# A graph attention layer on one core: edge blocks gathered once into a ring, sums scaled once a group, one-hots shared by two engines, own rows added later

## The chip, the cores and the metric

The kernel runs on one core of one Trainium2 chip. The metric is the device time of one execution in microseconds. The engines are PE (TensorE; PEld is its weight load), DVE (VectorE), ACT (ScalarE), POOL (GpSimd) and SP (SyncE, which here only starts transfers); each has an instruction queue of its own, and they meet at semaphores. A queue is named with a q behind the engine (DVEq: the register instructions of DVE's queue).

## The reference

```python
xn = layer_norm(x, ln1_g, ln1_b)                     # 6250 nodes, 256 columns
h = (xn @ W).reshape(N, 8, 32)
a_src, a_dst = einsum(h, att_src), einsum(h, att_dst)
src, dst = edges + (i, i) for every node i           # 100000 sorted by dst, and the node's own row
e = leaky_relu(a_src[src] + a_dst[dst], 0.2)
ee = exp(e - segment_max(e, dst)[dst])
agg = segment_sum(h[src] * ee / segment_sum(ee, dst)[dst], dst)
out = layer_norm(agg + xn @ W_res + bias, ln2_g, ln2_b)
x = x + out + gelu(out @ ffn_w1 + ffn_b1) @ ffn_w2 + ffn_b2
x = x + top-2-of-8 experts(layernorm(x))             # weights from softmax(x @ Wr + br)
```

The destinations are drawn as 6250 u^2 with u uniform, so the low-numbered nodes have most of the edges.

## The kernel before, in words

There are four stages, one behind the other: the node stage (norm, `h`, the table `node_table` of 272 columns per node: eight heads of 32 values and a one, and eight `a_src`), the edge stage, the layer (merge, second norm, the two products of the small network, routing, the rows sent to the experts' buffers) and the experts. Only the first three are touched.

The edge stage works on the 391 blocks of 256 sorted edges (NEB). A block's destinations lie in windows of 128 nodes (49 of them, NT); a block that reaches into a further window is handled again for that one. One block with one window is a step; there are 440 steps in 55 groups of eight (GS, NG), and the steps come in order. For each step POOL gathers the block's 256 source rows as two indirect transfers of 128 rows (L768) into one of four group buffers `gath`. The other engines turn in a round, one group each time. The iteration of `edges_dve` with number g does on DVE: the node chain of g (new maxima of the eight windows, the split of the values into `parts`), woven with the eight sums of group g-1: the sum in `win_mem` is scaled (L1044), then PE's product of one-hot and message is added (L1048). Then a piece of the expert weights is split (L1140), the scan over group g+1's scores (L1059, L1061) is made, the scores of g (L1066 to L1070), and the messages of g: gathered rows times weights (L1023), in pieces of four tiles; the last four tiles follow one by one among the sums. ACT copies `a_src` out of the gathered rows (L855), makes the one-hots (sixteen L862, L865), turns the places into the other one-hot (L868, L872), takes the exponentials (L889) and widens the one-hot (L897). PE does the sums (L957), a residual product (L834, L835), the spread of node values to edges (L926) and the maxima (L944).

A sum starts from the node's own row of the table, which lies in `win_mem` from the node stage.

In the layer, a batch is four windows of 128 nodes (two smaller ones at the end, 13 batches). POOL's queue holds for each batch b the root of the merged rows two batches on (L418), the eight row transfers of batch b-2 (L1346), and the root of the new rows (L1335). DVE turns that root into factors (L1508), ACT applies them (L1270) and then goes on with the gelus of the next batch (L1260, L1261), for which PE has three banks.

A value load reads a number out of the memory into a register of an engine's queue; it is a TENSOR_LOAD followed by FUSED_REGOPS and SEQ_ASSERT. `edges_dve` has one in each round (L966), whose number holds the eight windows of the group.

## Time and profile before

| | |
|---|---|
| time, median of 3 runs | 2292.91 us (2291.22 to 2293.44) |
| the profiled execution's own time | 2291.67 us |
| its span, first to last instruction | 2290.4 us |
| mean granted TensorE clock | 0.856 |
| node stage, edge stage, layer, experts (by the trace) | 0 to 96, 96 to 1252, 1252 to about 1620, to 2290 us |

The difference between the span and the profiled execution's time is 1.3 us and stays. Busy shares are a mean over stages with different limits, so the stages are read one at a time. A shift of a few us in 2292.91 is about what a measurement tells from nothing.

### The profile page before, as it was taken

What the parts mean: (1) busy time and instruction counts of PE and PEld (TensorE: products, weight loads), DVE (VectorE), ACT (ScalarE), POOL (GpSimd) and SP (SyncE); (2) the same over time, 40 slices, a digit from 0 to 9 for tenths busy, and PEclk for the clock granted to TensorE, in tenths of its full rate; (3) what the DMA queues carried; (4) which work ended last, traced back from release to release, by engine and by line L of the source; (5) the groups of instructions that cost most, each with busy time, mean ns of one, the idle gap of its engine ahead of it and who ended that gap; (6) DMA issues with size and microseconds to landing.
All of it is one profiled execution on the core that took longest, in us unless ns stands there. A gap on an engine that the chain in (4) does not pass through costs nothing.

```text
span 2290.4 us, 43652 instructions
## 1 busy us (share of the span) xinstructions
PE 1796.5 (78%) x12962; PEld 1538.9 (67%) x12962; DVE 1745.3 (76%) x5414; ACT 1556.3 (68%) x3225; POOL 1184.8 (52%) x1168
## 2 busy tenths in 40 slices
PE   6537666676666677766666899999399999999998
PEld 4425545555545455555544788889399999999997
DVE  7349999899899899989998788887455555555554
ACT  3366777777677777676772787887377766666675
POOL 3377777777777777777770134445222222222223
PEclk9857777777777777777777999999699999999999
DMA  7867666767666667766664223322835356436432
GB/s 228 209 184 215 215 210 197 207 216 215 214 205 203 208 214 215 225 200 200 204 207 136 74 91 98 101 78 75 253 48 122 48 118 159 87 48 158 85 48 38
DMA packets 283231, 358.12 MB, mean 156 GB/s; under 512 B 118629, under 2 KB 227006, under 8 KB 280562
## 3 DMA queue, kind: packets, MB, share of 16 engines
q1 hardware_dynamic: 218578, 202.63, 28.7%
q0 software_dynamic: 63840, 151.61, 26.0%
q8 instruction: 104, 1.70, 0.3%
q10 hardware_dynamic: 576, 1.09, 0.2%
q14 instruction: 133, 1.09, 0.1%
HBM read 464.93 MB, written 95.79 MB: 245 GB/s over the span
## 4 chain that ended last, share of the span: by engine, by line
PE 46%; POOL 21%; issue 11%; DVE 11%; ACT 6%; DMA 4%; DVEq 0%; SPq 0%; POOLq 0%; ACTq 0%
POOL edge_mem L768 21%; PE bank L1156 8%; PE bank L1144 7%; PE bank L1145 7%; PE bank L1146 7%; PE bank L957 6%; PE bank L1155 4%; DMA edge_mem<-node_table,src_col 3%; ACT edge_mem L862 3%; DVE layer_rounded L1140 1%; PE bank L1153 1%; ACT edge_mem L868 1%; DVE edge_mem L1023 1%; PE bank L523 1%; PE bank L834 1%
## 5 line engine op out<-in xcount | busy, mean ns | idle before, releaser
L768 POOL DMA_INDIRECT edge_mem<-node_table,src_col x880 | 840.5, 955 | 277.2 <-issue 261.7
L957 PE MATMUL bank<-edge_mem 128*128 128x264 f32 x1760 | 524.1, 459 | 6.3 <-ACT edge_mem L897 3.3
L957 PEld LDWEIGHTS bank<-edge_mem 128*128 128x128 f32 x1760 | 382.9, 226 | 110.1 <-issue 26.3
L1886 POOL DMA_INDIRECT out<-expert_mem,slot_tok x112 | 174.4, 1557 | 488.4 <-DVE expert_mem L1823 468.5
L1873 ACT ACTIVATE expert_mem<-bank,par 128x256 f32<-128x256 f32 x448 | 221.8, 495 | 187.6 <-PE bank L1146 187.5
L1140 DVE TENSOR_TENSOR expert_rounded<-expert_mem,expert_rounded 128x512 fp32r<-128x512 f32 x280 | 193.6, 691 | 194.6 <-ACT expert_rounded L1873 121.9
L1023 DVE TENSOR_TENSOR edge_mem<-edge_mem,bank 128x1056 f32<-128x1056 f32 x385 | 293.9, 776 | 7.5 <-ACT bank L889 1.7
L1156 PE MATMUL bank<-expert_rounded 128*128 128x512 f32 x784 | 278.8, 395 | 0.0
L1144 PE MATMUL bank<-expert_rounded 128*128 128x256 f32 x896 | 254.6, 284 | 27.1 <-DVE expert_rounded L1140 27.1
L862 ACT ACTIVATE edge_mem<-iota,dst_col 128x128 bf16<-128x128 bf16 x880 | 262.8, 386 | 0.0
L1145 PE MATMUL bank<-expert_rounded 128*128 128x256 f32 x896 | 254.4, 284 | 0.0
L1146 PE MATMUL bank<-expert_rounded 128*128 128x256 f32 x896 | 254.3, 284 | 0.0
L855 ACT COPY asrc<-edge_mem 128x128 f32<-128x128 f32 x55 | 16.4, 298 | 308.8 <-DMA edge_mem<-node_table,src_col 308.8
L1873 ACT ACTIVATE expert_rounded<-bank,par 128x256 fp32r<-128x256 f32 x448 | 222.2, 496 | 0.0
L1155 PE MATMUL bank<-expert_rounded 128*128 128x256 f32 x784 | 218.5, 279 | 0.0
L926 PE MATMUL bank<-parts,edge_mem 128*128 128x16 bf16 x2640 | 77.8, 172 | 155.2 <-DVE parts L1015 155.2
L1048 DVE TENSOR_TENSOR win_mem<-win_mem,bank 128x264 f32 x440 | 187.2, 426 | 13.1 <-PE bank L957 12.5
L1144 PEld LDWEIGHTS bank<-expert_rounded 128*128 128x128 f32 x896 | 172.5, 193 | 27.4 <-issue 25.0
L1044 DVE TENSOR_TENSOR win_mem<-win_mem,bank 128x264 f32 x440 | 186.6, 424 | 4.5 <-issue 1.7
L926 PEld LDWEIGHTS bank<-parts,edge_mem 128*128 128x128 bf16 x2640 | 72.8, 101 | 170.1 <-DVE parts L1015 170.1
L1145 PEld LDWEIGHTS bank<-expert_rounded 128*128 128x128 f32 x896 | 172.6, 193 | 2.4
L1146 PEld LDWEIGHTS bank<-expert_rounded 128*128 128x128 f32 x896 | 172.6, 193 | 0.0
(245 smaller groups left out, 4240.6 us busy)
## 6 DMA issues: line engine op xcount, KB each, us to landing
expert_rounded<-split_w SPq DMA_DIRECT2D x114, 2048.0 KB
edge_mem<-step_place SPq DMA_DIRECT2D x55, 512.0 KB, 5.4
split_w<-piece_hi SPq DMA_DIRECT2D x72, 256.0 KB, 4.8
split_w<-piece_lo SPq DMA_DIRECT2D x72, 256.0 KB, 6.0
piece_full<-in_L_ffn_W SPq DMA_DIRECT2D x64, 256.0 KB
expert_mem<-expert_rows SPq DMA_DIRECT2D x224, 64.0 KB, 2.8
edge_mem<-node_table,src_col POOLq DMA_INDIRECT x880
node_table<-win_mem SPq DMA_DIRECT2D x12, 544.0 KB, 4.4
```

The source lines that it names most:

```text
L768: pool.indirect_dma_start(gath[g % NGB][:, t, :], None, node_table, bass.IndirectOffsetOnAxis(ap=src_col[:, k, t % 2:t % 2 + 1], axis=0)). ...
L862: ins = act.activation(o16[:, t, :], iota16[:, :], ACT.Abs, scale=-1.0, bias=dst_col[:, k, t % 2:t % 2 + 1])
L957: ins = pe.matmul(bank[4 + at % 3][:, 0:AGG], onehot[g % 2][:, 2 * k + j, :], gath[g % NGB][:, 2 * k + j, 0:AGG], start=(j == 0), stop=(j ...
L1023: dve.tensor_tensor(rows_, rows_, wgt[:, r, :].unsqueeze(3).to_broadcast([P, end - first_, HEADS, HC]), ALU.mult).then_inc(weighted, 1)
L1048: dve.tensor_tensor(acc, acc, bank[4 + at % 3][:, 0:AGG], ALU.add).then_inc(added, 1)
L1140: return eng.tensor_tensor(lo, full, hi.bitcast(F32), ALU.subtract)
L1144: pe.matmul(out_ap, s_hi, m_lo, start=start, stop=False)
L1145: pe.matmul(out_ap, s_lo, m_hi, start=False, stop=False)
L1146: return pe.matmul(out_ap, s_hi, m_hi, start=False, stop=stop)
L1155: pe.matmul(out_ap[:, 0:n], s_lo, high, start=False, stop=False)
L1156: return pe.matmul(out_ap, s_hi, both_, start=False, stop=stop)
L1873: ins = act.activation(d, bank[1 + m % 4][:, 0:SLOT], ACT.Gelu, bias=par[jf % 3][:, 2 * KC + m:2 * KC + m + 1])
```

## The change

- `gath` becomes a ring of 28 blocks (RB), found by tables that DVE makes in the node stage. A block is gathered once: 782 transfers in 98 quads of four blocks (QUAD), where there were 880. POOL reads from a table, before each quad from the eighth on, how many steps must have been weighted, and waits for that count.
- Messages go to a buffer of their own, `message`, step by step, since a block may be needed twice. DVE and ACT find a step's block by two words loaded for each group.
- A window's weights in a group are all made with the maxima after that group, so only the first window's sum is scaled, once a group. `win_mem` is set to zero at the start.
- DVE makes half of the one-hots (one comparison over eight tiles), ACT the other half.
- The own rows are read again from the table in the layer, weighted and added by `add_self`: batch 0 on DVE, the others on POOL.
- The source rows of the tables are loaded by plain transfers, not by four indirect ones; the first product's weights of the layer (`layer_w1`) are loaded after the last messages.

```diff
+    RB = 28
+    QUAD = 4
+    NQUAD = -(-NEB // QUAD)
...
-        gath = [part(i * GT * ROW, GT, ROW) for i in range(NGB)]
+        ring = part(0, 2 * RB, ROW)
+        message = part(2 * RB * ROW, GT, AGG)
...
+                dve.memset(rows_s[:, :, :], 0.0).then_inc(tables_made, 1)
...
-                    pool.indirect_dma_start(rows_s[:, c, :].bitcast(I32), None, src_rows, at).then_inc(rows_gathered, 16)
...
+                dve.wait_ge(pool_const, 13)
+                t = step(dve.tensor_tensor(block_of, block_of, win_row[:, :], ALU.subtract))
+                dve.wait_ge(dve_step, t)
+                t = step(dve.tensor_scalar(lap_of, block_of, float(-(-65536 // RB)), None, ALU.mult))
...
-            for g in range(NG):
-                if g == 2:
+            pool.wait_ge(tables_made, 5)
+            for q in range(NQUAD):
+                if q == 2 * GS // QUAD:
                     turned_all(pool)
-                for t in range(GT):
-                    if g >= 2 and t % QUART == 0:
-                        if t == QUART:
-                            pool.wait_ge(asrc_turned, g - 1)
-                        if t == 2 * QUART:
-                            pool.wait_ge(cand_turned, g - 1)
-                        if t == 3 * QUART:
-                            pool.wait_ge(maxima_made, g - 1)
-                    if g >= NGB and t % QUART == 0:
-                        pool.wait_ge(summed, GS * (g - NGB) + (GS // 2 if t < 2 * QUART else GS))
-                    k = g * GS + t // 2
-                    pool.indirect_dma_start(
-                        gath[g % NGB][:, t, :], None, node_table,
-                        bass.IndirectOffsetOnAxis(ap=src_col[:, k, t % 2:t % 2 + 1], axis=0)).then_inc(gathered[g % NGB], 16)
+                if q >= RB // QUAD:
+                    done = pool.value_load(reuse_at[0:1, q - RB // QUAD + 1:q - RB // QUAD + 2], min_val=1, max_val=NSTEP)
+                    pool.wait_ge(weighted, done)
+                    pool.sem_inc(pool_step, 1)
+                    pool.wait_ge(pool_step, q - RB // QUAD + 1)
+                if q >= 2:
+                    pool.wait_ge(gathered[q % 2], 32 * QUAD * (q // 2))
+                for j in range(q * QUAD, min((q + 1) * QUAD, NEB)):
+                    for i in range(2):
+                        pool.indirect_dma_start(
+                            ring[:, 2 * (j % RB) + i, :], None, node_table,
+                            bass.IndirectOffsetOnAxis(ap=src_col[:, j, i:i + 1], axis=0)).then_inc(gathered[q % 2], 16)
...
-                    if n >= 1:
-                        act.wait_ge(asrc_turned, n)
-                    act.copy(asrc[:, :, :, :], gb[:, :, :, AGG:ROW].rearrange("p k j h -> p j k h")).then_inc(asrc_ready, 1)
+                    slots = slot_words(act, n)
+                    if n < 2:
+                        for i in range(2):
+                            act.wait_ge(gathered[i], 32 * QUAD * (n + 1))
+                    else:
+                        landed = [act.value_load(landed_at[0:1, n, i:i + 1], min_val=1, max_val=32 * QUAD * NQUAD) for i in range(2)]
+                        for i in range(2):
+                            act.wait_ge(gathered[i], landed[i])
+                    if n >= 2:
+                        act.wait_ge(asrc_turned, n - 1)
+                        act.wait_ge(scored, n - 1)
+                    for k in range(GS):
+                        t = step_tile(slots, k)
+                        ins = act.copy(asrc[n % 2][:, :, k, :], ring[:, bass.ds(t, 2), AGG:ROW])
+                    ins.then_inc(asrc_ready, 1)
                     o16 = onehot16[n % 2]
                     if n >= 2:
                         act.wait_ge(maxima_made, n - 1)
                         act.wait_ge(oh_wide, n - 1)
-                    for t in range(GT):
+                    for t in range(GT // 2, GT):
                         k = n * GS + t // 2
                         ins = act.activation(o16[:, t, :], iota16[:, :], ACT.Abs, scale=-1.0, bias=dst_col[:, k, t % 2:t % 2 + 1])
                     ins.then_inc(act_step, 1)
                     act.wait_ge(act_step, n + 1)
-                    act.activation(o16, o16, ACT.Relu, scale=-1.0, bias=ones[:, 0:1]).then_inc(oh_ready, 1)
+                    act.activation(o16[:, GT // 2:GT, :], o16[:, GT // 2:GT, :], ACT.Relu, scale=-1.0, bias=ones[:, 0:1]).then_inc(oh_ready, 1)
...
-            if k == 0 or piece_of(2 * k + 1) != piece_of(2 * k - 1):
-                pe.wait_ge(weighted, NM * g + piece_of(2 * k + 1) + 1)
+            if k % 2 == 0 and k < EARLY:
+                pe.wait_ge(weighted, GS * g + k + 2)
+            if k >= EARLY:
+                pe.wait_ge(weighted, GS * g + k + 1)
             if at >= 3:
                 pe.wait_ge(added, at - 2)
             for j in range(2):
-                ins = pe.matmul(bank[4 + at % 3][:, 0:AGG], onehot[g % 2][:, 2 * k + j, :], gath[g % NGB][:, 2 * k + j, 0:AGG],
+                ins = pe.matmul(bank[4 + at % 3][:, 0:AGG], onehot[g % 2][:, 2 * k + j, :], message[:, 2 * k + j, :],
...
+            def weigh(g, k, first_, end):
+                if k == 0 and first_ == 0:
                     dve.wait_ge(weights_ready, g + 1)
-                dve.tensor_tensor(rows_, rows_, wgt[:, r, :].unsqueeze(3).to_broadcast([P, end - first_, HEADS, HC]), ALU.mult).then_inc(weighted, 1)
+                if (g, 0) not in words:
+                    words[g, 0] = slot_words(dve, g)
+                t = step_tile(words[g, 0], k)
+                return dve.tensor_tensor(message[:, 2 * k + first_:2 * k + end, :].rearrange("p t (h c) -> p t h c", c=HC),
+                                         ring[:, bass.ds(t + first_, end - first_), 0:AGG].rearrange("p t (h c) -> p t h c", c=HC),
+                                         wgt[:, 2 * k + first_:2 * k + end, :].unsqueeze(3).to_broadcast([P, end - first_, HEADS, HC]), ALU.mult)
+
+            def early_messages(g, m):
+                for k in (2 * m, 2 * m + 1):
+                    weigh(g, k, 0, 2).then_inc(weighted, 1)
+
+            def late_message(g, i):
+                ins = weigh(g, EARLY + i // 2, i % 2, i % 2 + 1)
+                if i % 2 == 1:
+                    ins.then_inc(weighted, 1)
...
-                            messages(p, 3 + k)
+                            late_message(p, k)
                             next(small, None)
                         w = window(p, k)
                         acc = win[:, w, 0:AGG]
                         acc_h = acc.rearrange("p (h c) -> p h c", c=HC)
                         if at:
                             dve.wait_ge(added, at)
-                        t_scaled = step(dve.tensor_tensor(acc_h, acc_h, scale[:, k, :].unsqueeze(2).to_broadcast([P, HEADS, HC]), ALU.mult))
+                        if k == 0:
+                            t_scaled = step(dve.tensor_tensor(acc_h, acc_h, scale.unsqueeze(2).to_broadcast([P, HEADS, HC]), ALU.mult))
                         next(small, None)
-                        dve.wait_ge(dve_step, t_scaled)
+                        if k == 0:
+                            dve.wait_ge(dve_step, t_scaled)
                         dve.wait_ge(summed, at + 1)
...
+                    if n >= 2:
+                        dve.wait_ge(maxima_made, n - 1)
+                        dve.wait_ge(oh_wide, n - 1)
+                    targets = dst_col[:, n * GS:n * GS + GS // 2, :].rearrange("p k j -> p (k j)")
+                    dve.tensor_tensor(onehot16[n % 2][:, 0:GT // 2, :], iota16[:, :].unsqueeze(1).to_broadcast([P, GT // 2, P]),
+                                      targets.unsqueeze(2).to_broadcast([P, GT // 2, P]), ALU.is_equal).then_inc(oh_half, 1)
...
-                    dve.wait_ge(gathered[g % NGB], 16 * GT * (g // NGB + 1))
-                    t = step(dve.tensor_tensor(score[:, :, :], gb[:, :, AGG:ROW], b_edge[:, :, 0:HEADS], ALU.add))
+                    dve.wait_ge(asrc_ready, g + 1)
+                    t = step(dve.tensor_tensor(score.rearrange("p (k j) h -> p k j h", j=2), asrc[g % 2].rearrange("p j k h -> p k j h"),
...
+        def add_self(eng, b):
+            n = batch_tiles(b)
+            wv = win[:, tiles_before(b):tiles_before(b) + n, 0:AGG].rearrange("p t (h c) -> p t h c", c=HC)
+            sv = self_in[:, 0:n, :].rearrange("p t (h c) -> p t h c", c=HC)
+            ev = win[:, tiles_before(b):tiles_before(b) + n, AGG:ROW]
+            eng.wait_ge(own_weights, 1)
+            eng.wait_ge(self_loaded, 16 * (b + 1))
+            eng.tensor_tensor(sv, sv, ev.unsqueeze(3).to_broadcast([P, n, HEADS, HC]), ALU.mult).then_inc(self_used, 1)
+            eng.wait_ge(self_used, 2 * b + 1)
+            eng.tensor_tensor(wv, wv, sv, ALU.add).then_inc(self_used, 1)
...
                 if is_batch(b - 2):
                     dispatch(b - 2)
+                if b + 3 >= 1 and is_batch(b + 3):
+                    add_self(pool, b + 3)
                 if 0 <= b < NB - 1:
                     z_inverse_root(b, 0)
 
...
+                if b == 0:
+                    add_self(dve, 0)
+                dve.wait_ge(self_used, 2 * (b + 1))
+                yield
                 v(dve.reciprocal(rec[:, 0:n, :].unsqueeze(3), wv[:, :, :, HD:HC]))
```

Where an order is shown, a row is one instruction of that engine's queue, `ISA` and `REGISTER_ALU` are register instructions, and what it waits for stands in brackets.

DVE's queue from the end of one round's scores to its messages, before:

```order
L1070 TENSOR_TENSOR exponent<-exponent,bank 128x128 [waits dve_step]
L1074 TENSOR_TENSOR cand_rest<-bank,cand 128x128 [waits cand_high]
L1023 TENSOR_TENSOR edge_mem<-edge_mem,bank 128x4x264 [waits weights_ready]
L1079 TENSOR_TENSOR cand<-cand_rest,cand 128x16x8 [waits cand_middle]
L1023 TENSOR_TENSOR edge_mem<-edge_mem,bank 128x4x264 x2
```

and the same place of the change:

```order
L1187 TENSOR_TENSOR exponent<-exponent,bank 128x128 [waits dve_step]
L1191 TENSOR_TENSOR cand_rest<-bank,cand 128x128 [waits cand_high]
L760 TENSOR_LOAD slot_word [waits weights_ready]
L760 ISA x2
L760 TENSOR_LOAD slot_word
L760 ISA x2
L1105 REGISTER_ALU
L1105 ISA
L1105 TENSOR_TENSOR edge_mem<-edge_mem,bank 128x528
```

Two value loads now stand between the wait for the weights and the first message, and the message is two tiles, not four.

POOL's queue in the layer around one batch, before:

```order
L418 TENSOR_TENSOR rstd<-mv,neg_half 128x4 [waits m_stats]
L1346 DMA expert_rows<-win_mem,pos 53504x265 [waits gated,z_used,places_ready]
L1346 DMA expert_rows<-win_mem,pos 53504x265 x7
L1335 TENSOR_TENSOR z_rs<-z_arg,neg_half 128x2x3 [waits z_stats]
L1335 TENSOR_TENSOR z_rs<-z_arg,neg_half 128x2 [waits z_stats]
```

and the same place of the change, where `shared` is the buffer of the own rows:

```order
L436 TENSOR_TENSOR rstd<-mv,neg_half 128x4 [waits m_stats]
L1494 DMA expert_rows<-win_mem,pos 53504x265 [waits gated,z_used,places_ready]
L1494 DMA expert_rows<-win_mem,pos 53504x265 x7
L1452 TENSOR_TENSOR shared<-shared,win_mem 128x1056 [waits self_loaded,own_weights]
L1454 TENSOR_TENSOR win_mem<-win_mem,shared 128x4x264 [waits self_used]
L1483 TENSOR_TENSOR z_rs<-z_arg,neg_half 128x2x3 [waits z_stats]
L1483 TENSOR_TENSOR z_rs<-z_arg,neg_half 128x2 [waits z_stats]
```

The product and the sum of the own rows stand between the row transfers and the root of the new rows.

## Rows read from the trace of the kernel before

**Rows 1.** Stages, by windows: us, then busy us (instructions) of each engine, clock, DMA share.

```profile
core 0: us, PE busy (x) PEld busy (x) DVE busy (x) ACT busy (x) POOL busy (x), PEclk, DMA share, GB/s
160.00:1200.00 1040.00, 707.64 (x5459) 544.70 (x5458) 946.48 (x3165) 753.25 (x1415) 788.35 (x827) 0.76 0.69 209
1300.00:1590.00 290.00, 285.29 (x2033) 260.52 (x2032) 239.91 (x788) 230.19 (x402) 117.09 (x110) 0.99 0.27 87
```

**Rows 2.** The gathers by line: duration ns min/median/max, first and last start us.

```profile
L768 POOL DMA_INDIRECT edge_mem<-node_table,src_col x880: 942/946/1421, 96.3 to 1203.6; - x176
```

**Rows 3.** Waits between 160 and 1200 us: us in total, times, longest.

```profile
ACT asrc L855 <- DMA edge_mem<-node_table,src_col: 269.3, 52, 7.3
DVE piece_lo L1140 <- ACT piece_hi L743: 40.2, 36, 2.9
```

**Rows 4.** One round on DVE, timeline: start us, us, instruction, idle before.

```profile
601.83 0.37 DVE L975 TENSOR_REDUCE whole<-bank 128x72 f32<-128x216 f32 x1
...
608.22 0.43 DVE L1048 TENSOR_TENSOR win_mem<-win_mem,bank 128x264 f32 x1
608.58 0.18 DVE L983 COPY old<-win_mem 128x16 f32 x1
608.78 0.43 DVE L1044 TENSOR_TENSOR win_mem<-win_mem,bank 128x264 f32 x1
609.13 0.16 DVE L986 TENSOR_TENSOR win_mem<-win_mem,newm 128x8 f32 x1
...
612.76 0.41 DVE L1048 TENSOR_TENSOR win_mem<-win_mem,bank 128x264 f32 x1
...
617.64 1.25 DVE L1023 TENSOR_TENSOR edge_mem<-edge_mem,bank 128x1056 f32<-128x1056 f32 x1
```

**Rows 5.** The same round on PE: the last six sums of the group.

```profile
605.53 5.61 PE L957 MATMUL bank<-edge_mem 128*128 128x264 f32 x24
```

**Rows 6.** The round's value load on DVE's queue, by line.

```profile
L966 DVEq TENSOR_LOAD <-win_word x55: 299/304/558, 135.6 to 1221.6; - x55
L966 DVEq FUSED_REGOPS  x55: 190/190/216, 136.2 to 1221.9; - x55
```

**Rows 7.** DVE groups by form, 160 to 1200 us: busy us, mean ns.

```profile
L1023 DVE TENSOR_TENSOR edge_mem<-edge_mem,bank 128x1056 f32<-128x1056 f32 x153 | 186.9, 1249 | 6.4 <-ACT bank L889 0.8
L1023 DVE TENSOR_TENSOR edge_mem<-edge_mem,bank 128x264 f32<-128x264 f32 x205 | 86.2, 421 | 0.2 <-issue 0.2
```

**Rows 8.** POOL at the end of the layer's third batch and behind it, timeline.

```profile
1335.48 1.38 POOL L418 TENSOR_TENSOR rstd<-mv,neg_half 128x4 f32<-128x4 f32 x1 [10.51 <-DVE mv L1486]
1337.05 1.07 POOL L1346 DMA_INDIRECT expert_rows<-win_mem,pos  x1 [0.19 <-issue]
...
1346.48 0.96 POOL L1346 DMA_INDIRECT expert_rows<-win_mem,pos  x1 [0.30 <-issue]
1347.75 1.35 POOL L1335 TENSOR_TENSOR z_rs<-z_arg,neg_half 128x6 f32<-128x6 f32 x1 [0.31 <-DVE z_arg L1502]
```

**Rows 9.** ACT behind it, timeline.

```profile
1349.34 1.59 ACT L1270 ACTIVATE layer_mem<-layer_mem,z_nm,z_rs 128x256 f32<-128x256 f32 x3 [2.12 <-DVE z_nm L1508]
1350.83 0.67 ACT L1260 ACTIVATE layer_mem<-bank,fb 128x512 f32<-128x512 f32 x1
1351.41 0.67 ACT L1261 ACTIVATE layer_hid<-bank,fb 128x512 fp32r<-128x512 f32 x1
```

**Rows 10.** PE there: first and nineteenth product of the next batch.

```profile
1348.17 0.40 PE L1144 MATMUL bank<-layer_rounded,layer_w 128*128 128x512 f32 x1
...
1352.29 0.39 PE L1144 MATMUL bank<-layer_rounded,layer_w 128*128 128x512 f32 x1
```

**Rows 11.** POOL's plain instructions in the node stage, timeline.

```profile
1.25 0.28 POOL L484 TENSOR_SCALAR_AFFINE_SELECT ident<-ident 128x128 f32<-128x128 f32 x1
...
8.38 0.93 POOL L575 IOTA win_shift<- 1x440 int32 x1
```

**Rows 12.** The layer's start, DVE and POOL, timeline.

```profile
1257.75 1.05 POOL L418 TENSOR_TENSOR rstd<-mv,neg_half 128x4 f32<-128x4 f32 x1 [3.36 <-DVE mv L1486]
...
1260.00 0.35 DVE L1473 RECIPROCAL rec<-win_mem 128x32 f32<-128x32 f32 x1
```

**Rows 13.** The node stage on DVE, timeline.

```profile
42.05 1.38 DVE L476 TENSOR_SCALAR edge_mem<-edge_mem,node_mv,node_root 128x256 f32<-128x256 f32 x4 [2.85 <-POOL node_root L498]
...
67.69 0.60 DVE L646 TENSOR_TENSOR win_delta<-win_row 1x440 int32<-1x440 int32 x1
```

**Rows 14.** DVE in the layer, by line: a product of two operands over 1024 columns.

```profile
L1517 DVE TENSOR_TENSOR layer_mem<-layer_mem 128x1024 f32<-128x1024 f32 (+2 forms) x13 | 15.1, 1164 | 0.4
```

More of the change, by code:

```diff
@@ L689, in build, with step_window, step_tile, slot_words @@
         QUART = GT // 4
[L690 to L695 removed]
+        EARLY = GS - 2
+        assert QUART == 2 * (GS - EARLY)
+        def step_window(words, k):
+            w = words & 63
+            if k:
+                w = w + ((words >> (3 + 3 * k)) & 7)
+            return nc.s_assert_within(w, 0, WIN - 1, skip_runtime_bounds_check_because="a step's window is at most WIN - 1")
+        def step_tile(slots, k):
+            return nc.s_assert_within((slots[k // 4] >> (6 * (k % 4))) & 63, 0, 2 * RB - 2, skip_runtime_bounds_check_because="a block's place in the ring")
+        def slot_words(eng, g):
+            return [eng.value_load(slot_word[0:1, 2 * g + i:2 * g + i + 1], min_val=0, max_val=(1 << 24) - 1) for i in range(2)]
         W_pieces = [[w[e].rearrange("(k p) c -> p k c", p=P) for e in range(E)] + [f.rearrange("(k p) c -> p k c", p=P)]
@@ L1075, in edges_dve @@
                 if 0 <= g < NG:
[L1076 removed]
+                    early_messages(g, 0)
                 if n < NG:
```

206 lines of the change are left out of this document (138 added, 68 removed).

## Prediction

> **What bounds the kernel now.** I read the windows by stage first: the edge stage lasts from 96 to 1252 us, half of the span, and in its steady part DVE is busy for 946 of 1040 us, POOL for 788, PE at a granted clock of 0.76; in the layer PE is busy for 285 of 290 us at 0.99 [rows 1]. Busy shares do not name the bound, so next the gathers by line: the first starts at 96.3 us and the last of 880 at 1203.6 [rows 2], one every 1107.3 / 879 = 1.26 us, and a group of 16 every 20.15 us. POOL issues without a hole, and the waits say who waits for it: ACT stands 269.3 us in 52 rounds for gathered rows before it copies `a_src` [rows 3]. So POOL's issuing sets the pace.
>
> How far is the next bound? DVE waits in the same stretch 40.2 us for ACT's pieces, which come late because ACT started late [rows 3]. 1040 us hold 51.6 rounds, so that is 0.8 us a round. A round that never waited for a gather would take DVE 20.15 - 0.8 = 19.35 us. This is the number on which the case turns: the gathers can give back at most 0.8 us a round before DVE's own round is the bound, so the DVE work that the change adds and removes decides, not the number of gathers.
>
> **Node stage.** In the tables DVE gets 16 small integer instructions: five on 440 columns at about 0.64 us from start to start (as the 0.60 us ones there [rows 13]), eleven on 440 down to 1 column at 0.2 to 0.6, together about 5.5 us, at a place where DVE's norms follow one another. Against it, four of eight indirect transfers leave POOL's queue ahead of the node roots; DVE waits 2.85 us for such a root [rows 13], and I take back 3.5 us. Sum +2, between -4 and +6. Zeroing `win_mem` (12936 columns, below 15 us at about 1 ns a column) lies under the first gathers and their landing; uncovered it would cost those 15 us.
>
> **Edge stage, DVE's round.** Term by term:
> - Seven of eight scalings go. A step without a message is now four instructions in 1.03 us (L1048 at 608.22 to L1044 at 608.78 and L986 at 609.13, next L1048 1.03 us after the first [rows 4]). Each scaling holds DVE 0.35 us, so 2.45 us could go. But the sums wait for PE: its last six steps take 5.61 us, 0.93 each, and end at 611.14 [rows 5], while DVE starts the last addition at 612.76 [rows 4]. DVE is 1.6 us behind PE, and only that can be won; the rewritten node chain has to run beside it (two maxima now follow one another with a wait and register work between), so I take 1.2. Bounds 0.8 and 1.6.
> - Half of the one-hots come to DVE: one instruction over 1024 columns with 32-bit targets, nearest to the 1164 ns of a two-operand product over 1024 columns [rows 14]. +1.1 (lowest 0.6, if it ran two columns at once).
> - Messages of four tiles become two of two. 264 columns take 421 ns and 1056 take 1249 [rows 7]: 0.15 us fixed, so three more instructions, part of which overlaps, are +0.2.
> - Two value loads stand between the wait for the weights and the first message. A load is 304 ns, its register work 190 and 23 more [rows 6], 0.6 us with the gaps. Today's load has no wait ahead and lies under the messages. The new ones cannot start before the exponentials are there, and nothing covers them: DVE has just done its last scores. Two are 1.2, and the register work of the first message 0.2: +1.4. Bounds 0 (if they were taken early after all) and 2. They also delay the split of the candidates, for which PE's maxima wait.
>
> DVE's round becomes 19.35 - 1.2 + 1.1 + 0.2 + 1.4 = 20.85 us. Over 54 rounds against 20.15: +38 us.
>
> On the value load there is a rule: the Trainium skill, "DMA: Bandwidth & Descriptors", in its table of figures, gives `tensor_load` a floor of about 600 ns. The row shows 0.3 for the instruction and about 0.55 with what follows [rows 6]; by the page the two loads would be 1.2 as well, and if its 600 ns were for the instruction alone, 1.8 and 30 us more in all.
>
> **Edge stage, POOL's round.** 782 gathers at 1.26 are 985 us. For each of the 91 quads from the eighth on POOL has a value load and a wait by register; no row shows one on POOL. I take what DVE's queue pays, 0.6 [rows 6], between 0 and 1.2: 55 us. 1040 us in all is less than 54 x 20.85 = 1126, so POOL no longer sets the pace on average. It does in the first seven groups, which lie in one window and have eight new blocks each: 20.15 + 1.2 = 21.3 us, seven times 0.5 = +3. ACT loses 8 of 16 comparisons and half of a 2 us pass, gains seven small copies and three or four loads, and stays below 20 us, hidden by its wait [rows 3]; were that cover gone, its 2 to 3 us of loads would be the next to show.
>
> **Layer, start.** The chain from the last addition goes through the first merge. DVE does the own rows of batch 0 there: two two-operand instructions over 1056 columns, 1.2 each [rows 14], +2.4. POOL can begin batch 1 only behind its root at 1257.75, which takes 1.05 [rows 12]; at 4.4 us (below) it ends 3.2 us after DVE wants to merge batch 1 (1260.00 [rows 12]), and the split that PE waits for is queued behind that. Sum +6. The later load of `layer_w1` is hidden: 2 MB at the stage's 209 GB/s [rows 1] are 10 us, and it is asked for in the middle of the last sums, so it is there when the root of batch 0 is taken, ahead of PE's first product; without that cover it would cost those 10.
>
> **Layer, batches.** POOL's two instructions per batch stand behind the eight row transfers and ahead of the root of the new rows. Today the last transfer ends at 1347.44 and the root starts at 1347.75, 0.31 us later, with DVE's operand just there [rows 8]. So POOL has 0.3 us of room. What 1056 columns cost on POOL no row shows. The nearest plain instructions are 0.28 us for 128 columns and 0.93 for 440 [rows 11], 2.1 ns a column; at that 2.2 us each, 4.5 with the wait between, less 0.3: 4.2 us late. Who waits? DVE's factors, then ACT, which stands for them already (2.12 us) and has the gelus of the next batch behind them [rows 9]. PE starts that batch at 1348.17 and wants the first of its three banks back at its nineteenth product, 1352.29; the two gelus that free it end at 1352.08 [rows 9, 10]. There is 0.2 us of room there, so nearly all of the 4.2 reaches PE. It happens in batches 5 to 12 (six of four tiles, one of three, one of two; batches 1 to 4 have no transfers ahead of them and fit into waits of 10 us [rows 8]): 6 x 4.2 + 3 + 2 = +30 us. Lowest 12 (1.2 us an instruction), highest 40.
>
> Against moving this work to POOL speaks the Trainium skill, "GPSIMD Engine Reference", Performance versus the Vector engine: an addition over 2048 columns takes 4497 ns there and 2293 on DVE. An estimate by that page is 2.3 us for 1056 columns; the layer's term would be 32 us.
>
> **Sum.** 2291.7 (the profiled execution's own time, 1.2 below the median of the runs) + 2 + 38 + 3 + 6 + 30 = 2371 us. I say 2370.
>
> **Rivals.**
> - Faster: the gathers decide. If the value loads of DVE were taken while it still works (their price 0), its round is 19.45, and if POOL's loads hide in the 0.3 us between two gathers, the stage is 985 + 45 us of start and end: 54 x (20.15 - 19.45) = 38 us less. It ends below the present time when the layer costs less than 38: with 12 there, 2291.7 + 2 - 38 + 6 + 12 = 2274. For it: POOL is the proven bound today. Against it: the order shows the wait in front of the load. It decides from a DVE round below 19.6 us. 15 in 100.
> - No change to speak of: the loads hide, but the layer costs its 30: 2291.7 + 2 - 38 + 36 = 2292. 7 in 100 around that.
> - The layer's addition is hidden, the round is as above: 2291.7 + 2 + 41 + 6 = 2341. It needs POOL's instructions below 0.5 us. 15 in 100.
> - PE's clock falls in the layer too. In the edge stage, where PE stands 332 of 1040 us, 6.4 a round, the granted clock is 0.76; in the layer, without such holes, 0.99 [rows 1]. Eight holes of 4 us could each put a stretch at half speed, some 4 us more each: 2371 + 32 = 2403. 10 in 100.
> - DVE and POOL stop one another. The Trainium skill, "SBUF — State Buffer", says that a DVE instruction with two inputs from SBUF and a POOL instruction that reads SBUF exclude each other. As a mechanism here: in batches 1 to 4 POOL's two instructions run beside DVE's work, and each would hold one DVE instruction for up to 2.2 us, 4 x 4.4 = 18 us, most of it in DVE's waits: 2380. It has 8 in 100 and lies in the range.
> - That the change is not what it says: a few blocks more or less change nothing here, since DVE is the bound.
>
> **How the numbers follow.** The forecast as worked out has 45 in 100, the rivals what stands with them. The range must leave out no more than 2 in 10: it reaches down past the case at 2341 to 2300 and up to 2403: 2300 to 2405. A measurement of this kernel tells a change from none at about 0.2%, 4.6 us. Slower by more 77 in 100, within it 5, faster 18.
>
> **What would show it.** The rounds of DVE in the edge stage (start to start of the reduction of the maxima) at 20.6 to 21.2, with about 1.4 us idle in each before the first message; POOL's gathers with holes, waiting for weighted steps; ACT's wait for gathers still there early and smaller late. In the layer the root of the new rows 4 us late from batch 2 on, PE's idle time before the fourth hidden product near 4 us, and the batch that much longer. Wrong it would be if the load of a register is overlapped, if POOL's two-operand instruction is much faster than its neighbours, or if PE's granted clock differs in either stage.

## The result, and the profile after

The changed kernel takes **2387.36 us** (median) against 2292.07 us of the kernel before in the same measurement: a ratio of 1.0415 with the 95% interval 1.0397 to 1.0433. The forecast was 2370, between 2300 and 2405. Slower was right, the size fell short by 17 us. In the profiled executions the difference is 2387.85 - 2291.67 = 96 us, against 78 forecast.

The windows of the two stages, with the columns of [rows 1]: the first is the steady part of the edge stage, the second the layer with its batches.

```profile
141.00:1180.00 1039.00, 676.51 (x5296) 527.07 (x5296) 867.39 (x2896) 648.65 (x1337) 711.73 (x736) 0.75 0.64 195
1330.00:1660.00 330.00, 296.89 (x1925) 264.98 (x1926) 244.77 (x745) 221.90 (x381) 145.01 (x119) 0.91 0.28 87
```

PE's granted clock is 0.75 in the edge stage, where it was 0.76, but 0.91 in the layer, where it was 0.99. Where the 96 us lie follows from three marks: the first gather, DVE's last addition to `win_mem`, and the last root of the new rows (`z_rs`).

```
us                                   before   after   difference
first gather                           96.3   100.7     +4.4
DVE's last addition behind it        1156.3  1176.0    +19.7
first z_rs behind that addition        40.5    61.5    +21.0
last z_rs behind the first            314.6   365.6    +51.0
from there to the end (experts)       682.8   682.8      0
```

The spans differ by the sum, 96 us.

DVE's reductions of the maxima (one a group) start on average 20.15 us apart before and 20.53 after. Single rounds after are 19.9 to 21.4 from the ninth on, but for the last two (19.4); among the first eight are some of 22 and 23.

The gathers by line, as [rows 2], and who waited (total us, times):

```profile
L832 POOL DMA_INDIRECT edge_mem<-node_table,src_col x782: 940/946/1981, 100.7 to 1204.1; - x196
...
  DVE edge_mem L1105: 111.0, 56
...
  ACT asrc L931: 88.2, 24
```

98 gathers are gone, but the last one starts no earlier (1204.1 against 1203.6): POOL now stands 111 us and waits for DVE's weighted steps, where in [rows 3] ACT had waited for POOL. The bound has changed hands, and the new holder is slower.

One round of DVE, timeline, as [rows 4]: the end of the scores and the first messages.

```profile
610.81 0.29 DVE L1187 TENSOR_TENSOR exponent<-exponent,bank 128x128 f32<-128x128 f32 x1
611.14 0.29 DVE L1191 TENSOR_TENSOR cand_rest<-bank,cand 128x128 f32<-128x128 f32 x1
612.94 1.32 DVE L1105 TENSOR_TENSOR edge_mem<-edge_mem,bank 128x528 f32<-128x528 f32 x2 [1.51 <-issue]
```

The longest hole of the round is the 1.51 us ahead of the first message, with no releaser (the others, in the node chain, are 0.38 us each): DVE's queue is busy with the two value loads (on it a load takes 303 ns, its register work 190 and a check 23).

The start of the layer on POOL, DVE and PE, timelines, as [rows 12]:

```profile
1293.04 1.96 POOL L1452 TENSOR_TENSOR shared<-shared,win_mem 128x1056 f32<-128x1056 f32 x1 [7.57 <-DMA shared<-node_table]
1295.08 2.41 POOL L1454 TENSOR_TENSOR win_mem<-win_mem,shared 128x1056 f32<-128x1056 f32 x1
...
1297.52 0.35 DVE L1625 RECIPROCAL rec<-win_mem 128x32 f32<-128x32 f32 x1 [10.75 <-POOL win_mem L1454]
...
1303.70 0.79 PE L1262 MATMUL bank<-layer_rounded,layer_w 128*128 128x512 f32 x1 [13.75 <-DVE layer_rounded L1258]
```

POOL could begin batch 1 when its root was done at 1285.5, but the rows of batch 1 were asked for only at 1288.14: there is one buffer for own rows, and SP's queue has the two stores of fillings ahead of that load. These stores themselves start only at 1286.80, when DVE has just finished writing the filling. Then DVE stands for POOL and PE for DVE.

An early batch, in which no row transfers stand in POOL's queue; DVE, POOL and PE:

```profile
1353.77 1.22 DVE L1668 TENSOR_TENSOR layer_mem<-layer_mem,layer_in 128x1024 f32<-128x1024 f32 x1
1355.03 2.87 DVE L1669 TENSOR_TENSOR layer_mem<-layer_mem 128x1024 f32<-128x1024 f32 x1
1357.93 3.37 DVE L1671 TENSOR_TENSOR layer_mem<-layer_mem,layer_in 128x1024 f32<-128x1024 f32 x1
...
1354.69 2.12 POOL L1452 TENSOR_TENSOR shared<-shared,win_mem 128x1056 f32<-128x1056 f32 x1
1356.89 3.32 POOL L1454 TENSOR_TENSOR win_mem<-win_mem,shared 128x1056 f32<-128x1056 f32 x1
...
1363.51 0.58 PE L1262 MATMUL bank<-layer_w,layer_hid 128*128 128x256 f32 x1 [4.08 <-DVE layer_mem L1687]
```

Three like instructions of `base` follow one another on DVE. The one that ran mostly alone takes 1.22 us, the two beside POOL's pair 2.87 and 3.37, and POOL's second takes 3.32 where it takes 2.45 undisturbed. DVE is 3.8 us late and PE stands 4.08. The ends show that the two take turns: POOL's first ends at 1356.81, DVE's second at 1357.90, POOL's second at 1360.21 and DVE's third at 1361.30. Each instruction of DVE ends 1.09 us behind the one of POOL that it overlaps. The same pair of long instructions (2.88 and 3.31 us) stands ahead of the first root, beside the pair of batch 3.

A later batch, with transfers ahead, as [rows 8 to 10]:

```profile
1429.83 0.96 POOL L1494 DMA_INDIRECT expert_rows<-win_mem,pos  x1 [0.30 <-issue]
1430.82 1.97 POOL L1452 TENSOR_TENSOR shared<-shared,win_mem 128x1056 f32<-128x1056 f32 x1
1432.87 2.47 POOL L1454 TENSOR_TENSOR win_mem<-win_mem,shared 128x1056 f32<-128x1056 f32 x1
1435.30 1.35 POOL L1483 TENSOR_TENSOR z_rs<-z_arg,neg_half 128x6 f32<-128x6 f32 x1
...
1436.89 1.58 ACT L1405 ACTIVATE layer_mem<-layer_mem,z_nm,z_rs 128x256 f32<-128x256 f32 x3 [6.34 <-DVE z_nm L1660]
...
1439.67 0.79 PE L1262 MATMUL bank<-layer_rounded,layer_w 128*128 128x512 f32 x1 [3.88 <-ACT layer_hid L1396]
```

The root starts 4.5 us behind the last transfer instead of 0.31; ACT's wait has grown from 2.12 to 6.34 us, and 3.88 us of it arrive at PE. DVE is held here too, without harm, as the root waits for POOL anyway: a small instruction of one operand takes 2.07 us where it takes 0.17 alone.

```profile
1430.76 2.07 DVE L1653 TENSOR_SCALAR z_arg<-mv 128x3 f32<-128x3 f32 x1
```

The windows of one such batch after and one before show what comes on top:

```profile
1435.00:1469.00 34.00, 29.74 (x192) 26.19 (x191) 25.08 (x75) 22.32 (x38) 16.16 (x14) 0.90 0.30 95
```

```profile
1430.00:1457.00 27.00, 26.62 (x189) 24.10 (x189) 23.10 (x75) 22.00 (x38) 11.43 (x11) 1.00 0.31 100
```

PE is busy for 29.7 instead of 26.6 us with the same products, because the granted clock is 0.90 instead of 1.00: behind its 3.9 us hole it runs at 1.2 instead of 2.4 GHz for a stretch. The products behind the hole start 0.43 us apart, and 0.23 later on:

```profile
1440.69 0.63 PE L1264 MATMUL bank<-layer_rounded,layer_w 128*128 128x512 f32 x1
1441.11 0.63 PE L1262 MATMUL bank<-layer_rounded,layer_w 128*128 128x512 f32 x1
...
1445.42 0.39 PE L1264 MATMUL bank<-layer_rounded,layer_w 128*128 128x512 f32 x1
1445.65 0.39 PE L1262 MATMUL bank<-layer_rounded,layer_w 128*128 128x512 f32 x1
```

### The profile page after: what moved, and what is told of

The parts are those of the page before. It is cut to its first block and busy times, and to the rows that moved or that the text cites. A ratio compares the mean times of both kernels' runs of the same rounds, so it can differ in the third digit from the quotient of the medians.

```text
span 2386.6 us, 47129 instructions
## 1 busy us (share of the span) xinstructions
PE 1810.9 (76%) x12962; PEld 1555.0 (65%) x12962; DVE 1724.0 (72%) x5216; ACT 1462.3 (61%) x3171; POOL 1152.2 (48%) x1093
## 3 DMA queue, kind: packets, MB, share of 16 engines
q10 hardware_dynamic: 576, 1.09, 0.1%
## 5 line engine op out<-in xcount | busy, mean ns | idle before, releaser
L832 POOL DMA_INDIRECT edge_mem<-node_table,src_col x782 | 756.0, 967 | 357.9 <-issue 236.9
L1105 DVE TENSOR_TENSOR edge_mem<-edge_mem,bank 128x528 f32<-128x528 f32 (+1 forms) x550 | 305.8, 588 | 96.7 <-issue 85.3
L1023 PE MATMUL bank<-cand,edge_mem 128*128 128x27 bf16 x880 | 32.3, 186 | 213.7 <-issue 212.2
L1159 DVE TENSOR_TENSOR win_mem<-win_mem,bank 128x264 f32 x440 | 187.5, 426 | 8.9 <-PE bank L1038 6.1
L1262 PEld LDWEIGHTS bank<-expert_rounded 128*128 128x128 f32 x896 | 172.8, 193 | 26.5 <-issue 24.0
L959 ACT CAST cand<-bank 128x128 bf16<-128x128 f32 x55 | 15.9, 290 | 263.9 <-PE bank L1010 263.9
L1263 PEld LDWEIGHTS bank<-expert_rounded 128*128 128x128 f32 x896 | 173.0, 193 | 2.4
L1264 PEld LDWEIGHTS bank<-expert_rounded 128*128 128x128 f32 x896 | 172.9, 193 | 0.0
L1023 PEld LDWEIGHTS bank<-cand,edge_mem 128*128 128x128 bf16 x880 | 28.1, 104 | 222.3 <-issue 222.3
L1274 PEld LDWEIGHTS bank<-expert_rounded 128*128 128x128 f32 x784 | 147.2, 188 | 29.9
L931 ACT COPY asrc<-edge_mem 128x16 f32 x440 | 88.1, 204 | 117.9 <-DMA edge_mem<-node_table,src_col 88.2
```

The lines of the kernel that those rows point to most:

```text
L832: pool.indirect_dma_start(ring[:, 2 * (j % RB) + i, :], None, node_table, bass.IndirectOffsetOnAxis(ap=src_col[:, j, i:i + 1], axis=0)).th ...
L1105: return dve.tensor_tensor(message[:, 2 * k + first_:2 * k + end, :].rearrange("p t (h c) -> p t h c", c=HC), ring[:, bass.ds(t + first_, ...
L1159: dve.tensor_tensor(acc, acc, bank[4 + at % 3][:, 0:AGG], ALU.add).then_inc(added, 1)
L1262: pe.matmul(out_ap, s_hi, m_lo, start=start, stop=False)
L1263: pe.matmul(out_ap, s_lo, m_hi, start=False, stop=False)
L1264: return pe.matmul(out_ap, s_hi, m_hi, start=False, stop=stop)
```

## The experiments

All are built from the changed kernel. Times are medians, ratios are to the kernel before, which took 2294 to 2295 us beside them and 2292 beside the changed kernel; so a difference of two medians holds to about 3 us. "First z_rs" is counted from DVE's last addition (61.5 us in the changed kernel), "layer" from there to the last z_rs (427.0), a "batch" from one z_rs to the next.

**All own rows on DVE.**

```diff
-                if b == 0:
-                    add_self(dve, 0)
+                add_self(dve, b)
...
-                if b + 3 >= 1 and is_batch(b + 3):
-                    add_self(pool, b + 3)
```

> Own rows of all batches added by DVE in its merge, none by POOL. My theory: the layer is 72 us longer than before because of POOL's two instructions (late root of the new rows behind them, and DVE held while POOL reads SBUF), so without them a batch falls from 32 to 34 us back to 28, with the product of two 2.4 us instructions a batch mostly in DVE's waits; the start stays some 18 us longer than before. Layer from the last addition to the last factor 427 -> about 380 us, total about 2340. Rival: the work costs the same wherever it stands, as DVE carries 2.4 us more in every batch: 12 x 2.4 = 29 us stay, total about 2365. Second rival: the layer is long because PE's clock fell and not because of POOL: then no change, 2387.

Measured 2342.27 us, 1.0203 [1.0186, 1.022]. Layer 380.9 us, first z_rs at 54.9, batches 28.8 us. So 46 of the 72 us that the layer had grown came through POOL's part; what stays is 14 us at the start and 1.5 us a batch. At the start DVE now stands itself for the rows of batch 1, 6.29 us. The first rival (29 us stay, 2365) fails, the second too: the clock rose to 0.97 in this stage (from 1330 to 1560 us), so its fall follows the holes and is no cause by itself.

```profile
141.00:1180.00 1039.00, 676.23 (x5311) 527.50 (x5312) 867.61 (x2898) 648.74 (x1338) 710.37 (x736) 0.75 0.65 195
1330.00:1560.00 230.00, 222.55 (x1510) 199.25 (x1509) 201.54 (x609) 175.07 (x303) 84.04 (x79) 0.97 0.33 104
```

**Batch 1's own rows asked for early.**

```diff
+            load_self(1)
             sp.wait_ge(filling_ready, 1)
...
-                if 1 <= b + 3 < NB:
+                if 2 <= b + 3 < NB:
```

> The own rows of batch 1 are asked for before the two stores of fillings instead of behind them, as soon as DVE has used batch 0's; all else as after. My theory: at the start of the layer POOL waits 7.6 us for these rows and DVE stands 10.8 us for POOL, with PE idle 13.8 us behind them. The load now goes out near 1281 us instead of 1288, so POOL ends near 1290 instead of 1297.5: 7 us less, total about 2380. Rival: the start is held by PE's clock, the weights or the residual rows queued behind; then at most 2 us.

Measured 2381.12 us, 1.0371 [1.0353, 1.0388]. POOL no longer waits for the rows, and first z_rs comes at 52.4 instead of 61.5, 9 us less; the layer is 420.2, 7 less. The edge stage of this execution ended 2.8 us later, in its first rounds, which this edit doesn't touch. The theory holds: 7 us were expected, and the medians differ by 6, the ratios by 10.

```profile
1287.19 1.05 POOL L436 TENSOR_TENSOR rstd<-mv,neg_half 128x4 f32<-128x4 f32 x1 [5.00 <-DVE mv L1639]
1288.22 1.95 POOL L1453 TENSOR_TENSOR shared<-shared,win_mem 128x1056 f32<-128x1056 f32 x1
```

**The value loads one round early.**

```diff
             def node_chain(g):
                 window(g, 0)
+                if g + 1 < NG:
+                    words[g + 1, 0] = slot_words(dve, g + 1)
```

> DVE takes its two value loads for a group's places in the ring one round early, behind the last messages of the group before, instead of behind its wait for the weights; all else as after. My theory: they are the 1.5 us in which DVE is idle before the first message of each round, so the rounds fall from 20.53 to about 19.2 us once POOL no longer limits (the first seven stay near 20.1): 54 x 1.35 less 7 = 66 us less, total about 2321. Rival: the time comes back as a wait of DVE for ACT, PE or the gathers (POOL's 782 gathers alone need 985 us, 18.2 us a round): half or less of it, above 2350. Second rival: the idle time is the landing of the weights and not the loads: no change.

Measured 2342.93 us, 1.0207 [1.019, 1.0225]: 44 us less, two thirds of what I expected. The timeline of a round of DVE shows the loads gone and a part of the hole left:

```profile
621.51 0.28 DVE L1193 TENSOR_TENSOR cand_rest<-bank,cand 128x128 f32<-128x128 f32 x1
622.18 1.32 DVE L1107 TENSOR_TENSOR edge_mem<-edge_mem,bank 128x528 f32<-128x528 f32 x2 [0.39 <-ACT bank L966]
```

1.51 us have become 0.39, in which DVE really waits for the exponentials: 1.1 us a round. The steady rounds are 19.4 us. The first eleven rounds stay at 21 on average (POOL's gathers and their landing), and some of the gain is lost there: on average 20.53 to 19.68. So the cause was right, and 0.4 us of the hole was the wait for the exponentials, which the loads had covered.

**Sums scaled in every step.**

```diff
-                        if k == 0:
-                            t_scaled = step(dve.tensor_tensor(acc_h, acc_h, scale.unsqueeze(2)...
+                        factor = scale if k == 0 else ones[:, 0:HEADS]
+                        t_scaled = step(dve.tensor_tensor(acc_h, acc_h, factor.unsqueeze(2)...
```

(`factor` is `ones` in the added steps, so nothing of the result changes.)

> The sums are scaled in every step again: in the steps 2 to 8 of a group by ones, so that the result stays the same; seven instructions of 128x264 more in each round of DVE. My theory, as in the prediction: of their 2.45 us 1.2 lay on the path, because PE's sums came later than DVE wanted them; DVE's round is now fuller, so putting them back costs between 1.2 and 2.45 a round: about +1.6 x 54 = 86 us, total 2473. Rival: DVE is the bound without any slack and all 2.45 count: +132, 2519. Second rival: they fit in DVE's waits for PE: below +30.

Measured 2462.57 us, 1.073 [1.0712, 1.0748]: +75 us, rounds 21.87 instead of 20.53, +1.34 each. Seven instructions of 0.35 us are 2.45, so 1.1 us of them are hidden. The prediction had 1.2 on the path. That is nearest to the +1.2 to 2.45 of my theory, and both rivals fail; but its reason, that PE's sums come later than DVE wants them, fails too. DVE's waits between 160 and 1180 us, in the changed kernel and then in this run:

```profile
DVE win_mem L1067 <- DVE win_mem L1067: 39.2, 100, 0.7
DVE win_mem L1159 <- PE bank L1038: 4.6, 21, 0.2
...
DVE win_mem L1158 <- PE bank L1038: 5.2, 11, 0.6
...
DVE win_mem L1067 <- DVE win_mem L1154: 1.2, 4, 0.3
```

DVE hardly stands for PE in either. It stands 0.8 us a round for itself: a window's maxima (L1067) wait for the maxima of the window before, and without a scaling between them nothing covers that. The scalings fill these holes, which is 0.8 of the 1.1 us.

**POOL's own rows behind the root.**

```diff
+                if 0 <= b < NB - 1:
+                    z_inverse_root(b, 0)
                 if b + 3 >= 1 and is_batch(b + 3):
                     add_self(pool, b + 3)
-                if 0 <= b < NB - 1:
-                    z_inverse_root(b, 0)
```

> POOL still adds the own rows of batches 1 to 12, but behind the root of the new rows instead of ahead of it. My theory has two causes: the root stands 4 us late behind POOL's two instructions, and DVE instructions with two inputs in SBUF are held while they run (1.2 -> 2.9 to 3.3 us beside them). The first is gone now, the second moves to the gelus' lower halves and the merge: a batch falls from 34 to about 32 us where transfers stand ahead, the early ones stay at 32; 8 x 2 = 16 us less, total about 2371. Rival A, the place in the queue is all: batches fall to 28, as when DVE adds the rows, total 2342. Rival B, the holding is all: no change or slower, 2387 and above.

Measured 2346.98 us, 1.0233 [1.0216, 1.025]: 40 us less with the same work on the same engine. Layer 387.2, first z_rs at 55.6, batches 29.1 us. I had expected 16; rival A's 45 is nearer. The holding is there and now hits small instructions of DVE:

```profile
1420.09 1.95 DVE L1660 SCALAR_TENSOR_TENSOR z_nm<-mv,z_rs 128x6 f32<-128x6 f32 x1 [1.48 <-POOL z_rs L1483]
1421.95 0.41 DVE L1687 TENSOR_TENSOR layer_mem<-layer_mem,bank 128x256 f32<-128x256 f32 x1
1422.29 0.18 DVE L1736 TENSOR_TENSOR place<-bank,filled 128x32 f32<-128x32 f32 x1
1422.50 0.16 DVE L1738 TENSOR_TENSOR filled<-filled,bank 128x8 f32<-128x8 f32 x1
1422.69 1.92 DVE L1740 TENSOR_TENSOR sel<-sel,place 128x64 f32<-128x64 f32 x1
...
1420.04 1.96 POOL L1452 TENSOR_TENSOR shared<-shared,win_mem 128x1056 f32<-128x1056 f32 x1
1422.08 2.45 POOL L1454 TENSOR_TENSOR win_mem<-win_mem,shared 128x1056 f32<-128x1056 f32 x1
```

The first and the last of DVE's take 0.17 and 0.23 us in the changed kernel. The three between them read one operand from a bank of PE's results (PSUM) and take 0.41, 0.18 and 0.16 us as there, though POOL's second runs beside them. DVE loses 3.5 us a batch here, about as much as the 3.8 in the early batches of the changed kernel, but at a place where DVE has time: only 1.8 of it shows. So what the pair costs depends on where in the batch it stands, both for the root behind it and for DVE beside it.

**All one-hots on ACT.**

```diff
-                    for t in range(GT // 2, GT):
+                    for t in range(GT):
...
-                    dve.tensor_tensor(onehot16[n % 2][:, 0:GT // 2, :], iota16[:, :]...
```

(With it go DVE's two waits ahead of it and the waits of ACT and PE for `oh_half`, and ACT's last pass covers all 2048 columns.)

> All one-hots are made by ACT again (sixteen comparisons and one pass over 2048 columns a group), none by DVE; all else as after. My theory: DVE sets the pace, ACT waits 5 us a round for PE's maxima, so taking the 1.22 us instruction from DVE shortens a round by 1.1 us as the prediction put it: 54 x 1.1 less about 7 for the first groups, in which POOL is the bound: 52 us, total 2335. Rival: ACT's 3.4 us more a round come late in the chain from the gathered rows through ACT's copies to PE's maxima, and DVE waits there instead: less than 20 us, above 2367.

Measured 2341.84 us, 1.0215 [1.0194, 1.0236]: 46 us less (expected 52). Rounds 19.66, steady ones 19.4. ACT carries 836 instead of 649 us in the same 1039 us and is hardly waited for (DVE stands 11.4 us for its pieces between 160 and 1180 us); the half on DVE was paid for nearly in full.

**Three edits together**, all own rows on DVE, the early request and the early value loads:

> Three edits together: own rows by DVE, batch 1's own rows asked for early, value loads one round early. My theory: they touch different stages and add up: 45 from the layer, 45 from the value loads, 2 to 4 for the early request (DVE needs it less than POOL): 2387 - 93 = 2294, the time of the kernel before. Rival: with DVE fuller in both stages one of them gives back 10 or more, above 2304.

Measured 2291.9 us, 0.999 [0.998, 0.9999]. Rounds 19.67, layer 374.7. They add up: the time of the kernel before, to 0.1%. First z_rs is at 47.1 us, where own rows on DVE alone had left it at 54.9 (the early value loads alone leave it at 61.4), and DVE no longer stands for the rows of batch 1. So 8 of the 14 us at the start were this load, more than the 2 to 4 expected of it here.

**The same and all one-hots on ACT:**

> As the kernel with the three edits, and all one-hots by ACT again. My theory: DVE's round falls from 19.4 to 18.3 us, and POOL's gathers need 18.2 on average: both are nearly the bound, so about 0.9 of the 1.1 us come through: 2294 - 48 = about 2246, faster than the kernel before by 2%. Rival: ACT (13.2 us busy a round, now 16.6) is late with its copies or with the weights, and the round stays at 19: 2275 or more.

Measured **2249.28 us**, 0.9811 [0.9795, 0.9828]: faster than both kernels. Rounds 18.85 on average, most between 17.7 and 18.9, some of 22 to 26 among the first thirty; last addition at 1187.9 (before 1252.6), layer 376.1.

```profile
L832 POOL DMA_INDIRECT edge_mem<-node_table,src_col x782: 940/946/1443, 100.2 to 1123.6; - x196
...
  DVE edge_mem L1105: 37.1, 51
```

The last gather starts 80 us earlier than before, and POOL waits 37 us for DVE instead of 111. Here the 98 gathers saved are worth something, as POOL is nearly the bound again: 880 gathers at 1.26 us would have lasted until 1207 us.

**Batches 0 to 4 on DVE, 5 to 12 on POOL.**

```diff
-                if b == 0:
-                    add_self(dve, 0)
+                if b <= 4:
+                    add_self(dve, b)
...
-                if b + 3 >= 1 and is_batch(b + 3):
+                if b + 3 >= 5 and is_batch(b + 3):
```

> Own rows of batches 0 to 4 by DVE, of 5 to 12 by POOL ahead of the root, as after. My theory: two causes in two places. Batches 1 to 4 have no transfers ahead; there POOL's two instructions hold DVE's (1.2 -> 2.9 and 3.3 us) while PE waits, and this goes: the first root of new rows comes 54.9 us after the last addition instead of 61.5, the next two batches take 28.8 us instead of 32.0. From batch 5 on the row transfers and the root's place decide, and those batches stay at 34. 6.6 + 6.4 = 13 us less, total about 2374. Rival: one cause (the place in the queue) holds for all batches; then the early ones, where POOL stands idle 10 us before the root, would not have been longer through POOL and taking it away gives nothing, 2387.

Measured 2376.8 us, 1.0356 [1.0338, 1.0375]. First z_rs at 54.8, the next batch 28.7 us, then 32.9 (batch 5's pair is ahead of its root, with row transfers before it), then 33.0, 33.1 and 34.0, much as in the changed kernel; layer 416.8, 10 us less. I had expected 13, with two batches of 28.8 us; only one lies between two roots without transfers ahead. In the early batches the three instructions of `base` take the same time again:

```profile
1347.48 1.21 DVE L1668 TENSOR_TENSOR layer_mem<-layer_mem,layer_in 128x1024 f32<-128x1024 f32 x1
1348.73 1.22 DVE L1669 TENSOR_TENSOR layer_mem<-layer_mem 128x1024 f32<-128x1024 f32 x1
1349.99 1.23 DVE L1671 TENSOR_TENSOR layer_mem<-layer_mem,layer_in 128x1024 f32<-128x1024 f32 x1
```

So there are two costs in two places, and the early one is no matter of the queue: POOL had stood idle for 10 us ahead of those roots. It is DVE and POOL holding one another. The batch from 32.0 to 28.7 us shows it by itself; in the 6.7 us at the first root lies also that a pair takes 2.5 us on DVE and 4.4 on POOL.

## Why the prediction was right, and where its sizes were not

The direction and the reason for it were right; that the total came within 17 us is partly luck. The edge stage was put 21 us too high, the layer 36 too low (15 at the start, 21 in the batches), the node stage 2 too low.

- **What bounds, and that DVE decides.** Right. POOL waits for DVE from the first laps on, and every edit that takes work from DVE's round shortens the kernel (the early loads, the one-hots), though POOL's gathers are untouched.
- **Node stage, +2.** Measured +4.4, close to the upper of its bounds (+6); no run divides it.
- **DVE's round, 20.85 us.** Measured 20.53 on average, so the term was +20 instead of +38 and +3. By its parts: scalings -1.2, shown at 1.34, but for another reason than the one given: it was to be PE's sums that let only part of the 2.45 be won, and it is DVE's chain of maxima, each waiting for the one before (39.2 us of waits, 4.6 for PE). That the size fits is luck; one-hots +1.1, shown at 0.87 on average and 1.1 in the steady rounds; value loads +1.4, where the hole is 1.5 and 1.1 of it came back. The split of the messages was not tried. The parts were each right within 0.3 and all erred in the same direction. With what the runs gave for them the round would be 19.9 to 20.2 us, so 0.3 to 0.6 of the 20.53 stay without a cause shown.
- **POOL's value load, 0.6 us a quad.** Wrong, without consequence: at 61 of these 91 places the interval from gather to gather is 1.24 to 1.30 us, as elsewhere. The others are longer and lie beside POOL's waits for DVE; what the loads add there isn't shown. DVE pays because a wait stands ahead of its loads.
- **Layer, start, +6.** Measured +21. This is the step that failed most: the prediction let POOL begin batch 1 behind its root, and did not follow the own rows' load through SP's queue. One buffer and two stores ahead of it cost 7 us of POOL's time (the early request brings back 9 at first z_rs). By the runs the 21 us are 6.6 that go when DVE adds the rows instead of POOL, 7.8 that go when their load is also asked for early, and 6.6 that stay.
- **Layer, batches, +30.** Measured +51. The mechanism for the late ones was right to the tenth where it was worked out (root 4.2 us late, as forecast; PE's hole 3.9, forecast nearly 4.2). What was missing is PE's clock: a batch is 34.0 us against 27.3, which is 6.7 = 3.9 of hole and 2.8 of slower products. The eight batches with transfers ahead are 3.6 to 6.8 us longer, 46 in all, against the 30 forecast.
- **"Batches 1 to 4 have no transfers ahead of them and fit into waits of 10 us".** This step failed: the one of them that lies between two roots costs 4.6 us, and the others lie in the start. The waits of 10 us are POOL's, and it was DVE that was late.
- **The rivals.** Two with 8 and 10 in 100 both came true in part beside the forecast: DVE and POOL stop one another (in the rows above DVE instructions go from 1.22 to 2.9 and 3.4 us), and PE's clock falls in the layer (0.91 instead of 0.99, about 2.7 us for each late batch, forecast 4 each). They had been treated as alternatives with a price each; they belonged into the sum. The Trainium skill, "SBUF — State Buffer", section "Who interferes with whom", says that a DVE instruction with at most one input in SBUF, outside the modes that use two ports, doesn't contend with POOL, and that `tensor_scalar` can enter such a mode. The trace agrees in that instructions with one of two inputs in a PSUM bank keep their 0.41, 0.18 and 0.16 us, and it has a `TENSOR_SCALAR` of one input held for 2.07 us; that this one ran in such a mode, no row shows. With both (18 and 32 us, by the prediction's own prices) it would have read 2421, too much by 34, since the edge stage was 21 us cheaper than thought and the prices of these two were set high.
- **"Faster: the gathers decide"** had its condition about right, a DVE round below 19.6 us: at 19.67 us (three edits) the kernel takes the time of the one before, at 18.85 it is faster (2249). It needed four moves that the change does not make.

Of the 14 us at the start of the layer that remain when DVE adds the own rows, 8 were the late load. The other 6.6 are open; DVE's three pairs ahead of the first root take 3 x 2.5 = 7.5 us, but no run shows that they are the reason.

## What to carry to other kernels

When a change saves work on the engine that sets the pace, first measure how far the next engine is: here 0.8 us of 20.15, so that everything the change gave to that next engine was paid for nearly in full, and the work saved was worth nothing until it was taken away again. A short addition to a queue costs by its place: with the same two instructions on POOL the layer is 72 us longer when they stand ahead of a root that others wait for, 32 when they stand behind it, and 26 with the work on DVE; the same value loads cost 1.1 us a round behind a wait and left no hole behind long instructions. For work moved to another engine follow its load through the queue that issues it as well.

## What the runs showed of the hardware

- DVE and POOL hold one another, turn by turn, while both work with two operands in SBUF: 128x1024 on DVE 1.22 -> 2.87 and 3.37 us, 128x64 0.23 -> 1.92 us, 128x6 0.17 -> 1.95; POOL's 128x1056 2.45 -> 3.32. DVE's `TENSOR_SCALAR` of 128x3, with one operand, is held too, 0.17 -> 2.07 us. DVE's sums with one operand in a PSUM bank are not (128x256 0.41, 128x32 0.18), nor are three `BATCH_NORM_STATS2` of one operand (1.08 us, half of it beside POOL).
- A product or sum of two operands over 128x1056 takes 1.96 to 2.47 us on POOL and 1.25 on DVE.
- POOL's value loads between gathers leave the interval of 1.25 us as it is at 61 of 91 places. Two on DVE directly behind a wait leave a hole of 1.5 us, and 1.1 of it goes when they are taken earlier, so 0.55 each.
- A hole of 3.9 us in PE's work is followed by a stretch at half clock (1.2 GHz): 2.8 us on 27 us of products; holes of at most half a microsecond (all own rows on DVE, 1370 to 1560 us) leave it at 0.97.
